# A transformer block on one core: values taken out by ScalarE, their bias folded through Wo, and four reorderings around it

## The reference

```python
h = _layernorm(x) * (1 + ca) + sa
q, k, v = [h @ W.T + b for W, b in (WQ, WK, WV)]        # 16 heads of 8
q, k = rope(q), rope(k)
attn = softmax(where(causal, q @ k.T / sqrt(8), -inf))
x = x + ga * ((attn @ v) @ Wo.T + Wo_b)
h = _layernorm(x) * (1 + cb) + sb
combine = the two best of 8 experts, their shares summing to 1
x = x + gb * sum_e combine[e] * (gelu(h @ w_fc[e] + b_fc[e]) @ w_proj[e] + b_proj[e])
```

## Time and profile before

| | |
|---|---|
| median of 3 runs | 536.73 us (536.02 to 537.96) |
| the profiled execution | 538.26 us, of which the span from first to last instruction is 536.5 |
| PE busy | 459.6 us (86%) |
| DVE busy | 397.1 us (74%) |
| ACT busy | 314.8 us (59%) |
| POOL busy | 327.9 us (61%) |
| step 0's first maximum on DVE; first matmul of the experts | 28.0 us; 350.8 us |
| transfers, mean | 127 GB/s |

### The profile page before, as it was taken

How to read it: one execution, slowest core, us unless ns; L and a number is a source line. 1 busy time by engine, 2 the same in 40 slices (tenths; PEclk the granted TensorE clock), 3 DMA queues, 4 the chain that set the end, 5 groups by cost and what they waited for, 6 DMA issues and landing times.

```text
span 536.5 us, 12559 instructions
## 1 busy us (share of the span) xinstructions
PE 459.6 (86%) x3543; PEld 336.3 (63%) x3543; DVE 397.1 (74%) x1198; ACT 314.8 (59%) x853; POOL 327.9 (61%) x465
## 2 busy tenths in 40 slices
PE   4478999899989989989989988789977879999980
PEld 3245565555655655655655654479876768999970
DVE  3678898799999999999999898834425633444684
ACT  4465666565555555555555555566656546887860
POOL 3144464556966966966966957834855673445781
PEclk9999999999999999999999999979999897999995
DMA  4335644545745745745746853422222232222744
GB/s 117 99 105 155 146 139 130 136 127 163 195 125 170 194 131 164 194 129 166 195 130 157 169 152 71 125 67 57 70 62 59 86 85 56 67 66 69 246 148 140
DMA packets 77987, 67.89 MB, mean 127 GB/s; under 512 B 10915, under 2 KB 71591, under 8 KB 77920
## 3 DMA queue, kind: packets, MB, share of 16 engines
q1 hardware_dynamic: 71696, 56.91, 40.7%
q0 software_dynamic: 4320, 8.47, 4.8%
q10 hardware_dynamic: 1904, 1.70, 1.0%
HBM read 25.47 MB, written 12.05 MB: 70 GB/s over the span
## 4 chain that ended last, share of the span: by engine, by line
PE 38%; DVE 31%; issue 14%; POOL 4%; ACT 4%; DMA 3%; another core or an unknown queue 3%; SPq 1%; DVEq 1%; ACTq 1%; POOLq 0%
DVE maxima L1429 8%; PE ps_sc L1608 8%; PE misc L1760 5%; PE misc L1598 4%; PE ps_pv L1714 4%; PE ps_max L1598 4%; PE ps_sc L1685 3%; DVE shifts L1443 2%; PE ps_max L1667 2%; ACT after_k L859 2%; DVE turned_a L1380 2%; DVE z L1039 2%; DVE stats L1024 2%; DVE low L1387 2%
## 5 line engine op out<-in xcount | busy, mean ns | idle before, releaser
L933 ACT ACTIVATE probs<-ps_sc 128x512 f32<-128x512 f32 x192 | 108.1, 595 | 61.6 <-PE ps_sc L1685 52.0
L1429 DVE TENSOR_REDUCE maxima<-ps_max 128x2 f32<-128x512 f32 (+1 forms) x192 | 130.2, 682 | 16.7 <-PE ps_max L1669 9.8
L751 POOL DMA_INDIRECT results<-after_k,after_e x71 | 70.0, 986 | 66.6 <-DVE after_k L1124 46.8
L1685 PE MATMUL ps_sc<-q_diags,k_stacks 128*128 128x512 f32 x192 | 97.4, 508 | 5.6 <-ACT probs L933 3.6
L761 POOL TENSOR_SCALAR_AFFINE_SELECT probs<-probs 128x512 f32<-128x512 f32 x128 | 81.6, 644 | 27.3 <-ACT probs L933 26.1
L1608 PE MATMUL ps_sc<-wproj_s,after_k 128*128 x568 | 81.0, 287 | 1.3 <-ACT after_k L859 0.7
L1608 PEld LDWEIGHTS ps_sc<-wproj_s,after_k 128*128 128x128 f32 x568 | 71.7, 198 | 5.9 <-issue 3.3
L711 POOL DMA_INDIRECT sorted_rows<-rows,slots x64 | 65.9, 1030 | 14.6 <-issue 10.0
L1124 DVE SCALAR_TENSOR_TENSOR after_k<-ps_sc,after_e,after_k 128x128 f32<-128x128 f32 x71 | 24.8, 349 | 64.3 <-PE ps_sc L1608 34.5
L1667 PE MATMUL ps_max<-k_diags,q_stacks 128*128 128x512 f32 x128 | 61.1, 478 | 2.1 <-DVE maxima L1429 1.9
L1117 DVE COPY after_k<-wfc_s 128x644 f32 x71 | 37.3, 528 | 25.9 <-issue 25.6
(11 more groups left out here) (180 smaller groups left out, 912.6 us busy)
## 6 DMA issues: line engine op xcount, KB each, us to landing
q_diags<-q_stacks SPq DMA_DIRECT2D x64, 128.0 KB
k_diags<-k_stacks SPq DMA_DIRECT2D x62, 128.0 KB
gate_now<-gate_rows SPq DMA_DIRECT2D x16, 320.0 KB
after_e<-sorted_rows SPq DMA_DIRECT2D x71, 65.0 KB
k_stacks<-high SPq DMA_DIRECT2D x32, 128.0 KB
q_stacks<-high SPq DMA_DIRECT2D x30, 128.0 KB
x_in<-in_x SPq DMA_DIRECT2D x16, 128.0 KB, 3.3
k_stacks<-low SPq DMA_DIRECT2D x16, 128.0 KB
```

The lines of the kernel that those rows point to most:

```text
L751: nc.gpsimd.indirect_dma_start(result_dram, bass.IndirectOffsetOnAxis(ap=row_in[m % RING][:, D + 1:D + 2].bitcast(U32), axis=0), y_out[m % ...
L933: nc.scalar.activation(probs[:, g % 2, c], ps_sc[u % 2][:], ACT.Exp, scale=SCALE).then_inc(S["exp_done"], 1)
L1429: nc.vector.tensor_reduce(to, of, AX, ALU.max).then_inc(S["max_done"], 1)
L1685: last = nc.tensor.matmul(ps_sc[u % 2][:].rearrange("p (w q) -> p w q", w=4), k_stack[(s.t + d) % 3][:, g, keys * P:(keys + 1) * P], q_dia ...
```

## The change

1. **Values.** From step 0 on ACT copies v out of its bank without a bias (`values_out`, slot 10, behind that slot's exponential). DVE does it once, for sequence 0, as a plain copy.
2. **Bias.** Before step 0 PE transposes v's bias (held alike in all partitions), DVE copies 16 columns out, PE multiplies them by Wo, and DVE adds Wo's bias. That sum takes the place of Wo's bias in the product with the gate.
3. **Spread.** SP issues k's spread ahead of q's low stack, and for sequence 0 all four of k's spreads; ACT issues none.
4. **Division.** In slot 0 DVE divides the heads before it takes the first maxima.
5. **Banks.** qr from 2 to 1, wo from 1 to 0, sh0 from 0 to 2.

```diff
-BANK = {'sh3': 1, 'attnT': 0, 'kr': 2, 'qr': 2, 'wo': 1, 'sh0': 0, 'sh1': 0, 'zT': 2, 'z2T': 1, 'v': 2,
+BANK = {'sh3': 1, 'attnT': 0, 'kr': 2, 'qr': 1, 'wo': 0, 'sh0': 2, 'sh1': 0, 'zT': 2, 'z2T': 1, 'v': 2,
         'router': 1, 'sh2': 0, 'heads0': 0, 'heads1': 1}
...
-                        for w in range(2 if s.t == -1 else 4):
+                        for w in range(4):
...
                 stack_q_high()
+                spread_k()
                 stack_q_low()
-                spread_k()
                 spread_q()
...
-                act_e.wait_ge(S["k_stacked"], 48)
-                act_e.wait_ge(S["ones_in"], 16)
-                act_e.wait_ge(S["cleared"], 4)
-                for w in (2, 3):
-                    at = slice(ROWS * w, ROWS * (w + 1))
-                    act_e.dma_start(k_diag[0][at, :, w, :].bitcast(F32), k_stack[0][at].bitcast(F32)).then_inc(S["k_spread"], 16)
...
+                def values_out():
+
+                    s.wait(act_e, S["v_mm"], 1, 1, 1)
+                    s.wait(act_e, S["pv_mm"], -1, 4, 4)
+                    if s.t == 0:
+                        act_e.wait_ge(S["zeroed"], 7)
+                        act_e.wait_ge(S["v_done"], 1)
+                    nc.scalar.activation(v_wide[(s.t + 1) % 2][:, :, :, 0:DK],
+                                         misc[BANK["v"]][:, 0:T].rearrange("p (a h d) -> p a h d", a=TILES, h=HEADS),
+                                         ACT.Copy).then_inc(S["v_done"], 1)
...
+                    if n == 10 and s.has(1) and s.t >= 0:
+                        values_out()
...
+                dve.wait_ge(S["bias_tr"], 1)
+                nc.vector.tensor_copy(bias_v, ps_max[0][:, 0:B]).then_inc(S["bias_turned"], 1)
                 dve.wait_ge(S["loaded_o"], 48)
+                dve.wait_ge(S["bias_mm"], 1)
+                nc.vector.tensor_tensor(bias_o, ps_max[0][0:B, D:2 * D], bo_s[0:B], ALU.add).then_inc(S["bias_added"], 1)
+                dve.wait_ge(S["bias_added"], 1)
                 dve.wait_ge(S["gate_done"], 3)
-                nc.vector.tensor_tensor(gate_row[:, 4 * D:5 * D], gate_row[:, 0:D], bo_s[0:B], ALU.mult).then_inc(S["gate_done"], 1)
+                nc.vector.tensor_tensor(gate_row[:, 4 * D:5 * D], gate_row[:, 0:D], bias_o, ALU.mult).then_inc(S["gate_done"], 1)
...
-                def values():
...
+                def first_values():
+
+                    dve.wait_ge(S["v_mm"], 1)
+                    dve.wait_ge(S["zeroed"], 7)
+                    dve.wait_ge(S["cleared"], 10)
+                    nc.vector.tensor_copy(v_wide[0][:, :, :, 0:DK],
+                                          misc[BANK["v"]][:, 0:T].rearrange("p (a h d) -> p a h d", a=TILES, h=HEADS)
+                                          ).then_inc(S["v_done"], 1)
...
+                    if n == 0 and s.has(-2):
+                        divide(0)
+                        divide(1)
                     if s.has(0):
                         maxima_of(n)
...
-                    if n == 10 and s.has(1):
-                        values()
+                    if n == 10 and s.t == -1:
+                        first_values()
...
-                    if n == 0 and s.has(-2):
-                        divide(0)
-                        divide(1)
...
+                        pe.wait_ge(S["bias_added"], 1)
...
+                    pe.wait_ge(S["mod_done"], 4)
+                    nc.tensor.transpose(ps_max[0][:, 0:P], bqkv_s[:, 2 * D:3 * D], ident_s[:]).then_inc(S["bias_tr"], 1)
+
+                def bias_through_output():
+
+                    pe.wait_ge(S["bias_turned"], 1)
+                    pe.wait_ge(S["loaded_o"], 48)
+                    nc.tensor.matmul(ps_max[0][0:B, D:2 * D], bias_v, wo_s[:], start=True, stop=True).then_inc(S["bias_mm"], 1)
```

More of the change, by code:

```diff
@@ L1803, in emit @@
                         gates()
+                    if n == 9 and s.t == -1:
+                        bias_through_output()
                     if s.has(0):
```

12 lines of the change are left out of this document (3 added, 9 removed).

## The result

| | before | after |
|---|---|---|
| median | 537.35 us, 4 runs (536.02 to 538.01) | 530.76 us, 4 runs (530.09 to 532.92) |
| ratio | | 0.988, 95% interval 0.985 to 0.992 |
| the profiled execution: time, span | 538.26, 536.5 us | 531.36, 529.3 us |
| PE's first maximum; start of the 192nd maxima on DVE | 26.61; 338.28 us | 25.92; 333.75 us |
| first matmul of the experts | 350.8 us | 346.2 us |

The change makes the kernel 6.6 us faster; the forecast was 531.1. How the 7.2 us of the two spans are made up is another matter. I took the start of each step's third maxima (slot 2) in both traces: it does not depend on where the division stands. After is ahead by 1.46 us in step 0, by 3.77 in step 4, by only 2.99 in step 14, by 4.30 in step 15 and by 4.53 at the last maxima.

What follows compares the result with a forecast made beforehand. Three level engines (DVE, PE, in short steps GpSimd) bound the steady steps, with late starts beside them. Terms 0.3 + 0 + 1.6 + 1.3 + 0.7 + 0.9 + 0.8 = 5.6 off 536.73 gave 531.1 us, range 526.8 to 535.2.

Steps and rivals of the forecast that it cites:

- Level engines at the turn of a step: Steady steps: DVE, PE and, in short steps, GpSimd finish level, so freeing one gains only what the others give.
- Values, 0.3: Loop: moving the addition frees 5.3 us of DVE, but only 0.3 counts, in step 4; ends 0 and 5.3.
- Start, 1.6: Ahead of 28 us: k's spreads all on SP, earlier clears and q's projection give 1.36 to 2.0 us, 1.6 taken.
- 2.29 more: Start: PE's first maximum follows the end of k's spread issues by 2.29 us, so at 25.25, 1.36 earlier.
- Spread, 1.3 + 0.7: Ends of steps 3 and 0: earlier k's spread removes waits of 1.3 and 0.7 us; nothing in other steps.
- Banks, 0.9: Early steps: q's projection no longer waits for k's turned products, 0.9 us; ends 0.5 and 3.2.
- Division, 0.8: Five pairs of steps: earlier division brings DVE's fourth and fifth maxima forward, 0.15 a pair, 0.8 us; ends 0 and 1.75.
- DVE alone: First rival: DVE bounds, so steps 4 to 14 gain 0.33 each; 526.9 us in all, chance 0.17.
- The port redealt: Second rival: DVE/GpSimd port waits vanish or spread, 5.5 us either side; 525.7 or 536.6 us, chances 0.08 and 0.12.
- Only the start gains: Third rival: spread stays held and early steps follow DVE; 1.6 and 0.2 remain, 534.9 us, chance 0.07.
- q's low stack late by a microsecond: Fourth rival: q's low stack lands 1 us too late, PE pays in 14 steps; slower, 545.1 us, chance 0.06.
- the forecast's case: Whole kernel: the forecast's own account holds, 528.7 to 532.8 us, chance 0.50.

Runs made afterwards that it cites:

- values on DVE: Changed kernel with the values copied out by DVE again from step 0 on, bias still through Wo: 534.10 us against the changed kernel's 531.29.
- two operations moved: Changed kernel with GpSimd's gate on Wo and gated bias onto the residual's input moved to DVE: 502.87 us against before's 517.52, ratio 0.972.
- the repeat: The changed kernel timed again, unedited, on another chip: 531.29 us against the kernel before's 539.21, ratio 0.984.
- early spread: Changed kernel with k's spread ahead of q's low stack only up to step 3, behind it from step 4: 531.48 us against the changed kernel's 531.29.
- late low part: Changed kernel with k's low part behind the fifth maxima in even steps from 4 on: 509.37 us against before's 516.75, ratio 0.986.

## Why the prediction was right, and where not

The time was met, 530.76 for 531.1, and that it was met so closely is luck in part: banks were worth three to four times their term, the division nothing, and the values part was no gain in the steady steps and, alone, a loss. These misses made each other good.

*What bounds.* Level engines at the turn of a step was right: 1.2 us more or less of DVE's busy time in a short step moves it by nothing (values on DVE). DVE idles before the second maxima, as I had said, though by 0.72 us and not by 0.33. It does not hold for the whole of a long step: there DVE's low part is on the path, and 0.6 us less of it made the step 0.6 shorter with PE's and GpSimd's work unchanged. The Trainium skill's Perfetto Trace Analysis, Optimizing Scalar/DVE Operations, says that moving work from a saturated DVE to ScalarE may make sense. By the rows of before that would have given up to 5.3 us; here it gave none in the steady steps, so a busy share of 95% and more did not show that DVE bounds.

*Values, 0.3.* In the steady steps 0, as argued. In step 14 it is 1.5 together with the other parts, and the reason stays open: alone it gives nothing there (19.63), and with the values back on DVE that step takes 19.60 although its low part is as short (0.57) as in the changed kernel. What the ends missed is a loss: alone the part cost 4.4 us, most of it by moving PE's code loading onto k's spread. The step that failed is that a copy hidden behind other work costs nothing; an edit also changes where every later load of code falls.

*Start, 1.6.* The third maxima came 1.46 earlier, but PE's first maximum only 0.69. The step that failed is "2.29 more": the fourth issue ended at 23.03 (four at the rate of the two end there and not at 22.96), and the first maximum started 2.89 us behind it. From the last issue's begin it is 3.5 us, with all four on SP, and 2.9 before, with the last on ACT; why, no run shows. The clears' share made it up.

*Spread, 1.3 + 0.7.* Step 3 gave 1.76 together with the banks, 1.28 alone. But a part of what it removed was chance: that spread's third issue, 1.87 us long, had one of queue 8's transfers beside it. The 0.7 of step 0 came only with the other parts (0.46 in all).

*Banks, 0.9.* Mis-sized: 2.8 us by undoing them, 4.0 alone, beyond my 0.9 and around the upper end of 3.2. The step that failed is the low end that I took: I held that most of PE's waits ahead of q's projection do not reach the end. In the early steps 2.1 us came of it, and 0.9 more ahead of step 0's third maxima, which I had counted with the start. The steady steps, which I called untouched, give 0.15 us in each short one, with q's projection no longer held by k's turned products.

*Division, 0.8.* Worth 0. The short steps' gain of 0.13 that it should have brought is there, and is the banks': they have it with the division behind the maxima, and lose it with the banks undone.

*Rivals.* DVE alone is refuted by the values on DVE. The port redealt, 0.20 in all, is what the steady long steps hang on: the change left it alone in four of five, and its banks lifted it in step 14. With what gain isn't clear: with the banks undone that step takes 18.98 with a low part of 1.43 us, and with the values back on DVE 19.60 with one of 0.57. The kernel with two operations moved shows the gaining end was real, 1.4 us a long step and more than my 1.1. The Trainium skill's SBUF — State Buffer, SBUF: two separate sides, has the port held for a whole instruction by whoever started first; the three lengths of one instruction, 0.41, 0.92 and 1.52 us, by where it falls against GpSimd's, agree. Only the start gains, and q's low stack late by a microsecond: neither came; the longest wait for q's low stack after is 0.2 us. Two slips of the sums change nothing: the forecast's case begins at 536.73 - 9.0 = 527.7 and not at 528.7, and the port's gain at 525.6.

*Not foreseen.* The two waits of GpSimd for row transfers, 1.4 us lost in one profile and half of it in the next. And 2.7 us behind the loop: 195.6 us from the 192nd maxima to the end, but 197.7 in the repeat and 198.2 before, so most of it is that one execution's and not the change's.

## What to carry to other kernels

Where several engines are level, look for the instruction that is sometimes three times its length, and at what another engine runs beside it, before moving work off the busiest engine: here 0.6 us of such a wait was worth 0.6 us a step, and 1.2 us of DVE's busy time nothing. Busy time can itself hold such waits, so it does not fall by an operation's own length alone. Give a transfer on which the next stage hangs some slack in the queue rather than the last place, since single issues and landings are late by over a microsecond at places that shifted here with edits elsewhere. And judge a small edit by the steps of the trace that it touches, not by the whole time alone, where such places can make 4 us of difference.

## What the runs showed of the hardware

**Code loading.** Queue 8 carried 31 transfers of 16 KB in each kernel, as the page of the values part alone has it:

```profile
q8 instruction: 31, 0.51, 0.5%
```

Near such a transfer an issue of SP took up to 2.2 us in place of 0.6, though not every time (beside 10 of 18 in the loop of before), and landings were late. Where PE waited for k's spread in the loop, it came 2.6 to 2.9 us after its last issue began if no such transfer was in flight (15 times in all programs), and 3.4 to 4.5 us if one was (7 times).

**Waits are not free.** 96 PE instructions that only waited for a semaphore already raised put the first matmul from 6.23 to 15.74 us; in the trace most start 0.106 us after the one before.

**The clock in step 0.** The granted clock fell to 0.50, the 1.2 GHz level, for 3.4 us in step 0 in some programs (before, the changed kernel and its repeat, values on DVE, division undone) and not in others (start or banks alone, early spread, banks undone, two operations moved, late low part). Repeat of the changed kernel, then the one with the late low part, whose order of work is the same up to there; the third number from the right is the clock:

```profile
36.00:42.00 6.00, 5.17 (x20) 3.32 (x19) 4.66 (x11) 1.82 (x4) 3.91 (x18) 0.72 0.61 159
```

```profile
36.00:42.00 6.00, 4.48 (x21) 2.67 (x21) 5.83 (x16) 2.69 (x6) 4.70 (x19) 1.00 0.60 156
```

PE had paused three times just before in both, for 0.7, 0.9 and 0.8 us (from 32.7 us on in the one, from 32.4 in the other); what made the difference, the traces do not show. Step 0 took 16.63 us in the one and 15.62 in the other, so a microsecond of step 0 between two profiles need not be the edit's. The gains in step 0 named above have this in them: before had the fall, the banks alone had not.

**Chips differ in one stage.** Steps of equal work are equally long on all chips, but the time from the 192nd maxima to the end was 195.6 to 198.3 us on the chips with a before of 537 and more, and 176.5 to 179.3 on the others. Waits of DVE and ACT from 340 us on in the changed kernel's repeat:

```profile
DVE after_k L1138 <- remote: 13.6, 4, 4.3
ACT x_in L867 <- remote: 13.2, 3, 7.2
```

In the profiles on the others, as that of the kernel with the division undone, neither row is there. What is remote in them I can't tell from the trace.
